# 64-wide attention: the transfers that put queries in place are issued by GpSimd on its own queue

## The reference

```python
def _L1_xattn_ref(input_Q, input_K, input_V, Wq, bq, Wk, bk, Wv, bv, Wo):
    B, S, D, H, DK = (4, 512, 256, 16, 64)
    def _proj(x, W, b):
        y = jnp.einsum('bsd,ed->bse', x, W) + b
        return y.reshape(x.shape[0], x.shape[1], H, DK).transpose(0, 2, 1, 3)
    Q = _proj(input_Q, Wq, bq)
    K = _proj(input_K, Wk, bk)
    V = _proj(input_V, Wv, bv)
    scores = jnp.einsum('bhqd,bhkd->bhqk', Q, K) / np.sqrt(DK).astype(np.float32)
    attn = jax.nn.softmax(scores, axis=-1)
    context = jnp.einsum('bhqk,bhkd->bhqd', attn, V)
    context = context.transpose(0, 2, 1, 3).reshape(input_Q.shape[0], -1, H * DK)
    return jnp.einsum('bse,de->bsd', context, Wo)
...
x = x + _L1_xattn_ref(_layernorm(x, axis=-1), ctx_1024, ctx_1024, L1_xattn_Wq, ...)
```

## Time and profile before

| | |
|---|---|
| median of 3 runs | 1706.48 us (1703.46 to 1710.64) |
| the profiled execution | 1718.63 us, span 1716.8 us |
| TensorE (PE) | 1434.2 us busy, 84% |
| VectorE (DVE) | 1066.3 us, 62% |
| ScalarE (ACT) | 828.5 us, 48% |
| GpSimd (POOL) | 492.2 us, 29% |
| queue q1 (SyncE) | 132.34 MB, 26.1% of the 16 engines' span |
| queue q0 (GpSimd) | 27.01 MB, 7.3% |
| queue q10 (ScalarE) | 8.65 MB, 1.6% |
| a placement transfer | 128 KB, 2.4 us from issue to landing |

### The profile page before, as it was taken

How to read it: one execution, slowest core, us unless ns; L and a number is a source line. 1 busy time by engine, 2 the same in 40 slices (tenths; PEclk the granted TensorE clock), 3 DMA queues, 4 the chain that set the end, 5 groups by cost and what they waited for, 6 DMA issues and landing times. The chain is left out here.

```text
span 1716.8 us, 29073 instructions
## 1 busy us (share of the span) xinstructions
PE 1434.2 (84%) x9522; PEld 1150.3 (67%) x9522; DVE 1066.3 (62%) x2423; ACT 828.5 (48%) x1944; POOL 492.2 (29%) x426
## 2 busy tenths in 40 slices
PE   3899874999999569999999975899585995888885
PEld 3566542888888558888888853699463884655553
DVE  4677643666666537666666656444376744687776
ACT  1466542544445337666666753455233451454541
POOL 2111011577777500000000013555203312134343
PEclk8899866999999879999999997899787996798987
DMA  4322124455565456544445522122450002221110
GB/s 127 128 85 83 51 99 172 114 156 146 130 164 135 69 126 142 125 119 121 115 117 134 123 95 85 62 78 75 142 183 28 1 0 68 77 71 63 63 46 25
DMA packets 139972, 169.27 MB, mean 99 GB/s; under 512 B 20001, under 2 KB 131617, under 8 KB 137313
## 3 DMA queue, kind: packets, MB, share of 16 engines
q1 hardware_dynamic: 115504, 132.34, 26.1%
q0 software_dynamic: 16032, 27.01, 7.3%
q10 hardware_dynamic: 8336, 8.65, 1.6%
HBM read 76.18 MB, written 24.12 MB: 58 GB/s over the span
## 5 line engine op out<-in xcount | busy, mean ns | idle before, releaser
L1090 ACT ACTIVATE a_probT<-a_t 128x512 f32<-128x512 f32 x256 | 151.7, 601 | 173.5 <-PE a_t L823 145.8
L904 DVE TENSOR_REDUCE a_nmax<-a_s 128x2 f32<-128x512 f32 x256 | 171.0, 685 | 103.5 <-PE a_s L819 103.1
L63 POOL TENSOR_TENSOR a_rstd<-a_veps,minus_half 128x2 f32<-128x2 f32 x32 | 22.8, 713 | 565.0 <-DVE a_veps L57 565.0
L819 PE MATMUL a_s<-a_ka,a_qa 48*128 48x256 f32 x512 | 124.3, 345 | 46.5 <-DVE a_nmax L904 22.8
L432 DVE TENSOR_REDUCE a_nmax<-a_score 128x2 f32<-128x512 f32 x128 | 88.2, 689 | 104.2 <-PE a_score L329 101.7
L819 PEld LDWEIGHTS a_s<-a_ka,a_qa 48*128 48x128 f32 x512 | 79.3, 204 | 107.3 <-issue 60.5
L1609 POOL DMA_INDIRECT x_rows<-f_hn,f_scatter_row x60 | 129.8, 2164 | 16.4 <-issue 16.4
L515 ACT ACTIVATE a_prob<-a_score,a_nmax 128x256 f32<-128x256 f32 x256 | 120.2, 481 | 23.4 <-DVE a_nmax L432 22.7
L823 PE MATMUL a_t<-a_qa,a_ka 50*128 50x256 f32 x512 | 124.2, 341 | 2.2 <-DMA a_qa<-a_m_lo 1.2
L524 ACT COPY a_probT<-a_T 128x512 f32<-128x512 f32 x128 | 75.8, 593 | 77.4 <-PE a_T L337 75.8
L1552 ACT ACTIVATE f_gate<-f_gate 128x512 f32<-128x512 f32 x64 | 38.3, 598 | 129.5 <-PE f_gate L1355 111.5
(11 more groups left out here) (375 smaller groups left out, 4342.4 us busy)
## 6 DMA issues: line engine op xcount, KB each, us to landing
area_odd<-in_L_experts SPq DMA_DIRECT2D x15, 1536.0 KB, 6.8
a_k_hi<-a_k_fresh_hi SPq DMA_DIRECT2D x128, 128.0 KB, 2.4
a_ctxT<-in_ctxT SPq DMA_DIRECT2D x64, 128.0 KB, 2.5
a_ka<-a_k_hi SPq DMA_DIRECT2D x128, 64.0 KB, 2.6
a_qa<-a_q_hi SPq DMA_DIRECT2D x128, 64.0 KB, 2.6
a_k_lo<-a_k_fresh_lo SPq DMA_DIRECT2D x64, 128.0 KB, 2.4
a_q<-a_q_fresh_hi SPq DMA_DIRECT2D x64, 128.0 KB, 2.4
a_q<-a_q_fresh_lo SPq DMA_DIRECT2D x64, 128.0 KB, 2.4
```

The costliest lines, as they stand in the source:

```text
L819: last_s = nc.tensor.matmul(ps_s[i][:, half, :], qa[rows, u % RING, j, half * P:(half + 1) * P], ka[rows, u % RING, j, :], start=True, sto ...
L904: nc.vector.tensor_reduce(nmax[:, u % 2, :, i * PPU + j], ps_s[i][:, :, :], AX.X, ALU.max, negate=True).then_inc(sem["nmax"], 1)
L1090: nc.scalar.activation(probT[:, t % NPT, i, :, :], ps_t[i][:, :, :], ACT.Exp).then_inc(sem["exp"], 1)
```

## The change

`place` becomes a function that takes the queue. SyncE places keys only. GpSimd places queries; its loop over the batches is written out, and in each batch the placements stand at the same steps as they did on SyncE, with `norm_rstd` of the next batch at step 1. The number of transfers, their sizes, sources, destinations and semaphores stay as they are.

```diff
--- before.py
+++ after.py
@@ -220,6 +220,17 @@
                 return sem["vb"], f * NV + i + 1
             return sem[what + "_lo"], f * NCH + (i + 1) * CPR
 
+        def place(queue, f, what, i):
+
+            queue.wait_ge(sem[what + "_lo"], f * NCH + (i + 1) * CPR)
+            hi, lo = fresh[what]
+            for half in range(2):
+                own, other = rows(half)
+                heads = slice(2 * CPR * i + half, 2 * CPR * (i + 1), 2)
+                copies = [(k_hi, own, hi), (k_hi, other, hi), (k_lo, own, lo)] if what == "k" else [(q2, own, hi), (q2, other, lo)]
+                for to, at, part in copies:
+                    queue.dma_start(to[at, heads, :].bitcast(F32), part[own, :, :].bitcast(F32)).then_inc(placed(f, what, i)[0], 16)
+
         block = ctx.enter_context(nc.Block())
 
         @block.sync
@@ -237,30 +248,18 @@
                 sp.dma_start(chip.x[:, s * GT:(s + 1) * GT, :], chip.x_rows.rearrange("(t p) d -> p t d", p=P)[:, s * GT:(s + 1) * GT, :]).then_inc(chip.x_back[s], 16)
             context(1)
 
-            def place(f, what, i):
-
-                sp.wait_ge(sem[what + "_lo"], f * NCH + (i + 1) * CPR)
-                hi, lo = fresh[what]
-                for half in range(2):
-                    own, other = rows(half)
-                    heads = slice(2 * CPR * i + half, 2 * CPR * (i + 1), 2)
-                    copies = [(k_hi, own, hi), (k_hi, other, hi), (k_lo, own, lo)] if what == "k" else [(q2, own, hi), (q2, other, lo)]
-                    for to, at, part in copies:
-                        sp.dma_start(to[at, heads, :].bitcast(F32), part[own, :, :].bitcast(F32)).then_inc(placed(f, what, i)[0], 16)
-
             def places(b, more, part=None):
                 for s in range(NU):
                     for name, f in rounds_at(s, b, more, delay=1):
-                        if name != "hT" and name[0] != "v":
-                            place(f, *name)
+                        if name[0] == "k":
+                            place(sp, f, *name)
                     if s == LAG + 2 and part is not None:
                         prefetch.part(sp, sem["wload"], part)
                     if s == CTX_STEP and b + 2 < B:
                         context(b + 2)
 
             sp.wait_ge(sem["zeros"], 1)
-            for what in "kq":
-                place(0, what, 0)
+            place(sp, 0, "k", 0)
             places(0, True)
             n = prefetch.beside(sp, sem["wload"])
             for b in range(1, B - 1):
@@ -566,8 +565,14 @@
             chip.sems.clear_last_stage(nc)
 
             norm_rstd(nc, pool, chip, sem, nb, TB, 0)
-            with pool.Fori(1, B) as f:
-                norm_rstd(nc, pool, chip, sem, nb, TB, f)
+            place(pool, 0, "q", 0)
+            for b in range(B):
+                for s in range(NU):
+                    if s == 1 and b + 1 < B:
+                        norm_rstd(nc, pool, chip, sem, nb, TB, b + 1)
+                    for name, f in rounds_at(s, b, b + 1 < B, delay=1):
+                        if name[0] == "q":
+                            place(pool, f, *name)
 
 
 def narrow_head_attention(nc, chip, stage, w, prefetch, late=(), x_rest=(), linear=None, out=None):
```

## The result

| | median of runs, us | runs | ratio to before [95% interval] |
|---|---|---|---|
| before | 1707.18 (1698.57 to 1722.73) | 20 | |
| after | 1721.66 (1711.9 to 1732.59) | 20 | 1.0079 [1.006, 1.0098] |

The kernel became slower, by 13.5 us by this ratio (10 to 17 by its interval; the two medians lie 14.5 us apart). The forecast was 1708 us, in a range of 1702 to 1719, and no difference that can be told. The profiled execution of the changed kernel took 1720.19 us (span 1718.4), only 1.6 us more than the profiled one of before. The profiled execution of before was a long one, 1718.63 us against a median of 1707.18, and its mean granted clock over the whole span was 0.90, against 0.92 in the changed kernel's. So I compare the stage itself. From the first `hT_lo` on VectorE to the start of the last addition to `x_tok` it took 417.95 us before and 429.24 after, 11.3 us more.

The account below looks back on a forecast made before the run. TensorE bounds the steady batches (busy 48.33 of 49.00 us), so gains lie only in start-up and batch 0. Terms 0.7 + 0.7 + 0 = +1.4 us, carried over to the 1706.5 us median, gave 1708 us, range 1702 to 1719.

Parts of the forecast that it names:

- the last sentence on the boundary: Steady batches: query placements other than those at the batch boundary have a step or more to spare; no cost.
- The shared DMA engines: Batch 0: query transfers beside `("k", 1)` make those keys land 0.4 to 1.0 us later; +0.7 us.
- GpSimd's pace: Time from one GpSimd query transfer's start to the next, taken as 1.28 us from the plain gather and scatter.
- my lower bound: Lowest pace allowed for GpSimd's transfers: SyncE's 0.65 us from start to start.
- First scores: Start-up: queries issued earlier but at a slower pace, so TensorE's first scores begin later; +0.7 us.
- My break-even: Start-up: the first scores neither gain nor lose at a GpSimd pace of 1.1 us; 0.65 gives -1.6 us.
- GpSimd is as quick as SyncE: Rival: first scores gain 1.6 us, perhaps 1.8 more, contention 0.7; -2.7 us, 1704 us; chance 0.08.
- The batch boundary: Batches 1 to 7: `norm_rstd` and ScalarE's `("q", 3)` wait behind query transfers but stay covered; 0 us.
- the threshold of 1.43: Batch boundary: GpSimd pace in us above which each boundary costs four times the excess.
- The rival that put the slow case here: Rival: a GpSimd pace near 1.87 us makes the batch boundary the wait; +16 us, 1722 us; chance 0.16.
- VectorE starves GpSimd: Rival: VectorE's normalising `TENSOR_SCALAR` stops GpSimd's descriptor work, pace 1.58 us at the boundary; +5.6 us, 1712 us; chance 0.08.

Follow-up runs that it names:

- experiment 8: The changed kernel run again, unaltered, beside new runs of the kernel before: 1721.9 us, ratio 1.0085.
- experiment 3: Kernel before, plus GpSimd issuing four transfers a query round of 128 runs of 64 bytes into a scratch tile: 1710.23 us, ratio 1.0015.
- experiments 5 and 7: 5: changed kernel mirrored, keys from GpSimd, queries from SyncE, ratio 1.005; 7: queries issued by ScalarE on its own queue, keys by SyncE, ratio 1.0269.

## Why the prediction was wrong

*The step that failed* is the last sentence on the boundary: "All other query placements of the steady batches have a step or more to spare; what ScalarE waits extra there lies beside a busy TensorE." The queries did have the time. But they are not what suffers: I asked for the slack of the transfers that move and not of those that they now run beside. The argument that I had made for `("k", 1)` of batch 0 (engines 86% busy with one queue, so a second one delays the keys) holds for `("k", 0)` and `("k", 1)` of every batch. The six steady periods with an excess of 1.4 us and more make 9.6 of the stage's 11.3 us.

*The shared DMA engines, +0.7 us in batch 0.* The mechanism was right, the size was not: this is the term of the sum that was too small. I let the keys be 0.4 to 1.0 us later; ScalarE's wait went from 5.51 to 8.02 us, 2.5 more, and the batch lost 1.7. In the changed kernel:

```profile
634.45 0.84 ACT L502 ACTIVATE a_k_fresh_hi<-a_proj,area_even 128x256 fp32r<-128x256 f32 x2 [8.02 <-DMA a_k_lo<-a_k_fresh_lo]
...
636.25 0.51 PE L315 MATMUL a_proj<-a_ctx_hi,area_odd_parts 128*128 128x256 f32 x2 [3.88 <-DVE a_k_fresh_lo L410]
```

The 2.5 us have two parts. SyncE's own issuing was held up (below), so that the last transfer of keys was issued 4.43 us after the first (630.62 - 626.19) where it had been 3.23 (628.01 - 624.78), 1.2 us more; and it landed 3.83 us after its issue where it had been 2.52, 1.3 more. I had two or three query transfers in before the keys' landing; at GpSimd's true pace it is all four, and four times the 0.56 us of the earlier trace rows are 2.2 us, near the 2.0 (steady) and 2.5 measured. By the Trainium skill (DMA: Bandwidth & Descriptors, Issuing engines are not separate DMA queues) the transfers of both issuers interleave on the same engines. The trace agrees, with these two numbers; I drew on the rule for one place and not for the others where it held as well. For `("k", 2)` I took nothing, and ScalarE's wait there grew too, from 4.55 to 5.28 us.

Not all of batch 0's 1.7 us is TensorE standing still. The whole batch, before and after:

```profile
603.25:651.25 48.00, 34.41 (x196) 29.77 (x197) 21.50 (x57) 18.59 (x53) 0.70 (x1) 0.80 0.50 120
```

```profile
604.70:654.42 49.72, 35.61 (x195) 31.10 (x196) 21.50 (x57) 18.48 (x53) 10.24 (x17) 0.77 0.48 116
```

TensorE's idle time grew by 0.5 us only, from 13.6 to 14.1. The same matmuls kept it busy 1.2 us longer, at a mean clock of 0.77 for 0.80: after the wait of 3.88 us the clock went down (0.63 from 636 to 642 us, a mean of its two levels, where it was 1.00 before). This split is of one execution. In that of experiment 8, the same kernel, TensorE was busy 34.36 us at 0.80, as before the change, and batch 0 took 49.42 us: there its loss is all idle time.

*GpSimd's pace.* I took 1.28 us from the indirect transfers; it is 0.58 from start to start, faster than SyncE's 0.65 and below my lower bound. The time of the indirect transfers was no measure of these plain ones.

*First scores, +0.7 us.* TensorE's wait was 7.64 us for 7.77; from the low parts of `("q", 0)` to the scores 5.9 us instead of 6.0. My break-even said that a pace of 0.65 gives 1.6 us back. It did not:

```profile
612.42 0.72 POOL L232 DMA_DIRECT2D a_q<-a_q_fresh_hi  x1 [10.64 <-DVE a_q_fresh_lo L410]
...
614.34 0.60 POOL L232 DMA_DIRECT2D a_q<-a_q_fresh_lo  x1
```

The fourth was issued at 614.34, 2.2 us after the low parts' end at 612.11, and not 3.4 as in the kernel before (614.09 - 610.66). But the scores began at 617.96, 3.6 us after it and not 2.55: beside the keys it landed later by what it was issued earlier. The ten transfers together ended no sooner for being issued by two. So the rival "GpSimd is as quick as SyncE" had the pace right and the gain wrong.

*The batch boundary, 0 us.* Right in its result. At 0.58 us the threshold of 1.43 is far away:

```profile
836.72 0.59 POOL L232 DMA_DIRECT2D a_q<-a_q_fresh_lo  x1
837.32 0.88 POOL L63 TENSOR_TENSOR a_rstd<-a_veps,minus_half 128x2 f32<-128x2 f32 x1
...
840.78 0.73 DVE L70 TENSOR_SCALAR a_hn<-x_tok,a_mv,a_rstd 128x256 f32 x2
```

`a_rstd` is ready 2.6 us before VectorE asks for it, and TensorE comes to the output product without a wait:

```profile
843.74 2.54 PE L358 MATMUL a_proj<-area_even,a_oT 128*128 128x256 f32 x11
```

The rival that put the slow case here had the right sign and about the right time (1722 us) by luck: its mechanism did not occur.

*VectorE starves GpSimd.* It did not: the longest of the 128 transfers took 0.72 us. A little went the other way, off the path: the normalising `TENSOR_SCALAR` takes 360 ns where it took 351, 360 with the small transfers of experiment 3, and 365 with all placements on GpSimd. By which mechanism, no run shows.

*What stays open:* why batch 1 waits longer than the others (3.92 us, then 2.8 to 2.9). It did so before the change as well, 2.12 us where the later ones waited 0.8, so the change added about as much there, 1.8 us. Open too is the rest between the 11.3 us of the stage in one execution and the 13.5 of the ratio, which lies within the interval, and whether the size of the packets has a part in the delay (experiments 5 and 7).

## What to carry to other kernels

A transfer that is moved to a queue of its own still takes its time on the DMA engines. Where one queue keeps them nearly busy (here 0.56 us of work for every 0.65 us issued), starting the less urgent transfers earlier makes the urgent ones late, here by 2.0 us for 2.2 us of work let in: ask who waits for the transfers that did not move, in every round in which both are in flight, and not only where a wait shows already. The wait that was 0.77 us once a batch, and free, became 2.8 us twice, and what the two exceeded their cover of about 4.25 us by lengthened the batch one for one. A second buffer behind the wait did more than any choice of queue.

## What the runs showed of the hardware

- A plain transfer of 128 KB in 128 runs of 1 KB takes GpSimd 0.59 us to issue, 0.58 from start to start, one of 8 KB in 128 runs as much, and one of 64 KB in 64 runs 0.54 to 0.55; the indirect gather, 0.97. It lands in 2.8 to 3.2 us (medians from 700 to 1000 us) beside SyncE's queue; the 8 KB ones land in 2.3.
- GpSimd's queue moves the same transfers in fewer, larger packets. From 628 to 634 us of the changed kernel (packets, MB, share of 16 engines), four transfers on `q0`:

```profile
q1 hardware_dynamic: 756, 0.68, 46.1%
q0 software_dynamic: 192, 0.52, 40.3%
```

  40.3% of 6 us is 2.4 us for the four, 0.60 each, against 0.56 for SyncE's alone and 0.53 for SyncE's in this window (46.1% of 6 us for 0.68 MB): the larger packets saved no engine time here.
- SyncE's issuing itself can be held up. In batch 0 of the changed kernel two transfers that take it 1.25 us took 2.46, and one of 0.61 took 1.29:

```profile
628.12 2.46 SPq L232 DMA_DIRECT2D a_k_hi<-a_k_fresh_hi  x2
630.62 1.29 SPq L232 DMA_DIRECT2D a_k_lo<-a_k_fresh_lo  x1
```

  A second queue is not needed for it: in the kernel before, the longest such issue took 2.07 us, with all placements on SyncE's queue:

```profile
636.88 2.07 SPq L249 DMA_DIRECT2D a_q<-a_q_fresh_lo  x1
```

- The medians from issue to landing hide all this: 2.4 us for the keys before and after. The transfers that ScalarE waits for are the last of a round, and in the two rounds with a wait these land 2.0 to 2.2 us later.
